# A cross-attention and mixture-of-experts kernel: the output bias added by VectorE instead of TensorE

## The chip, the core and the metric

The kernel runs on one core of one Trainium2 chip. The metric is the device time of one launch in microseconds (us). Engines are named as in the profile: PE is TensorE's matmuls and PEld its weight loads, DVE is VectorE, ACT is ScalarE, POOL is GpSimd, SP is SyncE. "L542" is line 542 of the kernel.

## The reference, cut to what matters

```
# x (8, 256, 256); ctx (8, 120, 256); 16 heads of 16; 8 experts
x = x + xattn(layernorm(x), ctx, ctx, ...)     # attention, ends in  out @ Wo.T + bo
x = x + ffn(layernorm(x), ...)                 # each row goes to one of 8 experts

def xattn(query, key, value, ..., Wo, bo, ...):
    ...
    out = einsum('bhqk,bkhd->bqhd', attn, v).reshape(Bq, Tq, D)
    return out @ Wo.T + bo

def ffn(x, router_w, router_b, expert_w, expert_b):
    logits = hs @ router_w + router_b
    ...                                        # argmax picks the expert, its softmax value is the gate
    out = gate * (hs @ expert_w[idx] + expert_b[idx])
```

The change is about `bo`, a vector of 256 floats, the same for every row.

## The kernel before

Eight batches b of 256 rows go through one software pipeline. Rows lie on the 128 partitions, so a batch is two tiles (TH = 2) of 128 rows by D = 256. Every engine runs its own instruction list, written out by hand, over iterations i = -1 to 7 with eight steps f = 0 to 7 in each. In iteration i four batches are in work: A = i + 2 (first layernorm, queries, keys, values), M = i + 1 (row maxima of the scores), i itself (scores, exponential, product with the values) and C = i - 1 (normalisation, output projection, residual), R = i - 2 (second layernorm, router). Engines wait for each other by semaphores: `v_mx` (DVE's maxima are done), `v_kL` and `v_qL` (the low parts of keys and queries), `p_op` (the output projection is in PSUM).

What one iteration does around the change, in the order of each engine:

- PE: step 4 scores (L500, L504), step 5 queries of A (L434), step 6 scores for the maxima of M (L474, L478), step 7 the values' product (L515), then `c_project(C)` (L542, L544), then `turn_max(M)` (L487, which waits for `v_mx`), the keys of the next batch (L434), the router's ranks; in the next iteration step 0 scores (L500, L504), step 1 `a_values` (L434, `w_nat,ctxs`, which waits for `v_kL`), and `c_out_turn` (L528).
- DVE: step 2 `maxima(M, 0)` (L1085), step 4 `ln1_stats(A + 1)` (L960, L963, L965), step 5 the router's logits (L1020 to L1030), `ln1_apply(A + 1)` (L979) and `queries_low(A)` (L1013), step 6 `maxima(M, 1)` (L1085), step 7 `route_choice`, `residual(C)` (L1103, then statistics L960 to L965), `keys_low(A + 1)` (L988), then small operations.
- POOL: powers -0.5 of the variances for both layernorms (`rsqrt1`, L338; `rsqrt2`, L362), and DMAs that scatter rows to their experts. In iteration -1 it also makes the bias operand (`output_bias`, L341 to L358), in iteration 1 it clears 4 tiles for the experts' bias (`bias_operands`, L328 to L332).

In iteration 7 `c_project(6)` stands in step 5, behind the scores. `c_project` puts two tiles into PSUM. An fp32 product is two matmul records in the trace for each of the two 128-row slices of the contraction (four L544 records for each tile), and ahead of them stands one bf16 matmul L542 with all ones as weights against `bo3`, whose rows 0, 32 and 64 hold the three bf16 parts of `bo`. DVE's L1103 adds the product to x in SBUF.

Behind the loop the last batches run mixed with the experts' blocks: 30 blocks of 128 rows, each read back from DRAM (SP), transposed (PE, L598), copied (ACT), multiplied (PE, L612, L614), gated (DVE, L1118) and stored by POOL's indirect DMA (L376). The projection of the last batch, `c_project(7)`, and its residual stand there, and POOL runs `store_block(0)` right before `rsqrt2(7)`.

Of the kernel before, what the change touches and what calls it, by code (L numbers as in the profile page):

```python
# [7 lines left out]
BF16 = mybir.dt.bfloat16  # L8
# [7 lines left out]
P = 128  # L16
# [4 lines left out]
def xattn_moe_kernel(nc, x, ctx_in, masks_in, Wq, Wk, Wv, Wo, bq_bk, bv, bo,  # L21
# [32 lines left out]
    with es:  # L54
# [56 lines left out]
        hT = sb("hT", [P, KC, T])  # L111
        utri = sb("utri", [P, P], BF16)
        onesb = sb("onesb", [P, P], BF16)
        bo3 = sb("bo3", [P, D], BF16)
        bor = sb("bor", [P, 2, D])
        tri8 = sb("tri8", [P, E, E])
        j128 = sb("j128", [P, E, NS])
        jblk = sb("jblk", [P, NBP[0]])
# [55 lines left out]
        for n in ("d_w0 d_w1 d_w2 d_w3 d_e d_bqk d_mk d_bv d_bias d_z0 d_z1 d_c0 d_c1 d_sc0 d_sc1 d_ebs d_ebp "  # L174
                  "c_pool c_late c_ebp c_warm c_dve a_T a_mk a_kbH a_kbL "
                  "g_r1 g_r2 p_xT p_q p_k p_v p_st p_pv p_mx p_T p_ot p_on p_op p_hT p_lg "
                  "a_tT a_xT a_qH a_kH a_exp a_oT a_hT a_hn a_le "
                  "v_ve1 v_xn v_qL v_kL v_va v_mx v_on v_x1 v_ve2 v_nb v_lc v_oh "
                  "a_ov g_bo p_rk v_slot v_be a_eb v_eb p_bT a_bT a_ob p_by v_by "
                  "dve").split() + [f"d_x{b}" for b in range(B)] + [f"d_hb{i}" for i in range(HR)] + [f"d_o{i}" for i in range(HR)]:  # L180
            s(n)

# [33 lines left out]
        def _(sp):  # L216
# [9 lines left out]
            sp.dma_start(rb_b[:, :], router_b.partition_broadcast(P)).then_inc(s("d_bias"), 16)  # L226
            sp.dma_start(eb[:, :], expert_b).then_inc(s("d_bias"), 16)
            sp.dma_start(r_nat[:, :, :], router_w.rearrange("(k p) e -> p k e", p=P)).then_inc(s("d_bias"), 16)
            for n in range(3):
                sp.dma_start(bo_b[32 * n:32 * n + 1, :], bo.rearrange("(o d) -> o d", o=1)).then_inc(s("d_bias"), 16)  # L230
            sp.wait_ge(s("d_w2"), 16)
            for b in range(2, B):
                load(b)
# [45 lines left out]
        def _(pool):  # L279
# [57 lines left out]
                    pool.wait_ge(s("v_xn"), b)  # L337
                pool.tensor_tensor(rs1[:, :], ve1[:, :], mhalf[:, :], ALU.pow).then_inc(s("g_r1"), 1)  # L338

            def output_bias():  # L340
                n = s("g_bo")  # L341
                pool.wait_ge(s("d_bias"), 16 * 6)
                pool.memset(bo3[:, :], 0.0).then_inc(n, 1)
                pool.wait_ge(n, 1)
                pool.tensor_copy(bo3[0:1, :], bo_b[0:1, :]).then_inc(n, 1)
                pool.tensor_copy(bo3[32:33, :], bo_b[32:33, :]).then_inc(n, 1)
                pool.tensor_copy(bo3[64:65, :], bo_b[64:65, :]).then_inc(n, 1)
                pool.wait_ge(n, 4)
                pool.tensor_tensor(bor[32:33, 0, :], bo_b[32:33, :], bo3[32:33, :], ALU.subtract).then_inc(n, 1)
                pool.tensor_tensor(bor[64:65, 0, :], bo_b[64:65, :], bo3[64:65, :], ALU.subtract).then_inc(n, 1)  # L350
                pool.wait_ge(n, 6)
                pool.tensor_copy(bo3[32:33, :], bor[32:33, 0, :]).then_inc(n, 1)
                pool.tensor_copy(bo3[64:65, :], bor[64:65, 0, :]).then_inc(n, 1)
                pool.wait_ge(n, 8)
                pool.tensor_tensor(bor[64:65, 1, :], bor[64:65, 0, :], bo3[64:65, :], ALU.subtract).then_inc(n, 1)
                pool.wait_ge(n, 9)
                pool.tensor_copy(bo3[64:65, :], bor[64:65, 1, :]).then_inc(n, 1)
                pool.wait_ge(n, 10)  # L358

            def rsqrt2(b):  # L360
                pool.wait_ge(s("v_ve2"), b + 1)
                pool.tensor_tensor(rs2[:, tiles(b)], ve2[:, :], mhalf[:, :], ALU.pow).then_inc(s("g_r2"), 1)  # L362
# [19 lines left out]
            for i in ITER:  # L382
                A, C = i + 2, i - 1
                if i == -1:
                    late_constants()
                if 0 <= i - 3:
                    scatter(i - 3)
                if A + 1 < B:
                    rsqrt1(A + 1)
                if i == -1:  # L390
                    output_bias()
                if i == 1:
                    bias_operands()
                if 0 <= C < B:
                    rsqrt2(C)
# [18 lines left out]
        def _(pe):  # L414
# [120 lines left out]
            def c_project(b):  # L535
                pe.wait_ge(s("a_oT"), b + 1)
                if b == 0:
                    pe.wait_ge(s("d_w3"), 16)
                    pe.wait_ge(s("c_late"), NLATE)
                    pe.wait_ge(s("g_bo"), 10)  # L540
                for h in range(TH):
                    pe.matmul(PJk[:, h, :], onesb[:, :], bo3[:, :], start=True, stop=False)  # L542
                    for k in range(KC):
                        t = pe.matmul(PJk[:, h, :], oT[:, k, h * P:(h + 1) * P], w_nat[:, 3, k, :],  # L544
                                      start=False, stop=(k == KC - 1))
                t.then_inc(s("p_op"), 1)

            def c_hidden_turn(b):
# [3 lines left out]
            def c_logits(b):  # L552
                pe.wait_ge(s("a_hT"), b + 1)
                if b == 0:
                    pe.wait_ge(s("d_bias"), 16 * 6)
                if b >= 1:
                    pe.wait_ge(s("v_lc"), b)
                    pe.wait_ge(s("v_slot"), b)
                if b == FB[1]:
                    pe.wait_ge(s("v_be"), 2)  # L560
                for h in range(TH):
                    t = full(RT_LG[:, h, :], lambda k: hT[:, k, h * P:(h + 1) * P], lambda k: r_nat[:, k, :])
                t.then_inc(s("p_lg"), 1)

            def r_ranks(b):
                pe.wait_ge(s("v_oh"), b + 1)
                if b >= 1:
                    pe.wait_ge(s("v_slot"), b)
                for h in range(TH):
                    t = TH * b + h  # L570
                    pe.matmul(RT_RK[:, h, :], utri[:, :], oh[:, t, :], start=True, stop=False)
                    m = pe.matmul(RT_RK[:, h, :], onesb[:, :], cum[:, place_in_cum(t), :], start=False, stop=True)
                if b + 1 in FB:
                    m = pe.matmul(RT_TOT, onesb[:, :], cum[:, place_in_cum(t) + 1, :], start=True, stop=True)
                m.then_inc(s("p_rk"), 1)
# [162 lines left out]
        def _(act):  # L738
# [108 lines left out]
                a.then_inc(s("a_kbL"), 1)  # L847

            def split_expert_bias():
                act.wait_ge(s("d_bias"), 16 * 6)  # L850
                act.activation(ebs[:, 0, :], eb[:, :], ACT.Copy).then_inc(s("a_eb"), 1)

            act.dma_start(w_nat[:, 1, :, :], Wk).then_inc(s("d_w1"), 16)
# [87 lines left out]
        def _(v):  # L941
# [32 lines left out]
            def ln1_apply(b):  # L974
# [5 lines left out]
                                        ALU.subtract, ALU.mult)  # L980
                i.then_inc(s("v_xn"), 1)

            def keys_low(bn):
                v.wait_ge(s("a_kH"), KC * (bn + 1))
                if bn >= 2:
# [114 lines left out]

            def residual(b):
                v.wait_ge(s("p_op"), b + 1)
                v.tensor_tensor(xr[:, tiles(b), 0:D], xr[:, tiles(b), 0:D], PJk, ALU.add).then_inc(s("v_x1"), 1)  # L1103
                v.wait_ge(s("v_x1"), b + 1)
                if b >= 1:
                    v.wait_ge(s("v_nb"), b)
                ln_stats(b, st2, xr[:, tiles(b), C_MEAN:C_MEAN + 2], ve2, "v_ve2")
# [28 lines left out]
            for i in ITER:  # L1136
                A, M, C, R = i + 2, i + 1, i - 1, i - 2
                isA, isM, isS, isC, isR = (0 <= n < B for n in (A, M, i, C, R))
                for f in range(NF):
# [20 lines left out]
                    if f == 4:  # L1160
                        if i == -1:
                            maxima(M, 1)
                            values(A)
                        if A + 1 < B:
                            ln1_stats(A + 1)
                    if f == 5:
# [107 lines left out]
```

## Time and profile before

| | |
|---|---|
| time, median of 3 runs | 224.46 us (223.33 to 224.56) |
| the profiled execution | 221.88 us, of which the span of its instructions 220.0 us |
| granted TensorE clock, mean | 0.973 |
| busy: PE, PEld, DVE, ACT, POOL | 194.4, 135.8, 137.5, 124.6, 69.4 us |
| L542 (ones by bias parts) | 16 matmuls, mean record 277 ns |
| L544 (output projection) | 64 matmuls, mean record 380 ns |
| L1103 (residual add) | 8 instructions, mean 674 ns |

Matmuls overlap in the pipeline, so a record is longer than the time that a matmul takes from the next; the distance from start to start tells the latter. Idle time in square brackets is the time that the engine stood idle before an instruction, and what ended it. A group "x4" starts at the first of its four instructions and ends with the last.

### The profile page before, as it was taken

To read this page: it belongs to the slowest core of one execution; us is meant where nothing else is said; L and a number is where in the kernel's file an instruction comes from. 1 tells how busy PE (TensorE), PEld (TensorE's weight loads), DVE (VectorE), ACT (ScalarE), POOL (GpSimd) and SP (SyncE) were. 2 spreads that over 40 slices of the span, in tenths; PEclk is the share of its full clock that TensorE was granted. 3 is DMA by queue.
4 is the path that set the end of the run, shared out by engine and by line. 5 is a ranking of instruction groups with operands and counts; after the bars stand their busy time and mean duration, and the time that the engine had idled before them with its cause. 6 is when DMAs were issued, how large, how long until landed. Compare 5 with 4: busy or idle time off the path is not lost.

```text
span 220.0 us, 4891 instructions
## 1 busy us (share of the span) xinstructions
PE 194.4 (88%) x1656; PEld 135.8 (62%) x1656; DVE 137.5 (62%) x479; ACT 124.6 (57%) x273; POOL 69.4 (32%) x106
## 2 busy tenths in 40 slices
PE   7999898999999999999999899889698982799930
PEld 2757464666685766757668455556587671588720
DVE  4577756688668877985973774884757580223420
ACT  2575684584784676487477556376636370645810
POOL 7321810050110230131040040040164667466672
PEclk9999999999999999999999999999999999589995
DMA  6899500005000010010010000014850215551110
GB/s 215 276 347 354 173 1 3 3 3 197 4 0 0 4 51 0 0 53 0 3 50 0 3 24 27 0 48 114 227 151 7 102 55 172 144 153 47 60 40 0
DMA packets 14650, 17.12 MB, mean 78 GB/s; under 512 B 2687, under 2 KB 12958, under 8 KB 14625
## 3 DMA queue, kind: packets, MB, share of 16 engines
q1 hardware_dynamic: 11698, 10.67, 16.3%
q0 software_dynamic: 2208, 4.24, 5.4%
q10 hardware_dynamic: 720, 1.91, 2.4%
q8 instruction: 14, 0.23, 0.5%
q14 instruction: 10, 0.07, 0.1%
HBM read 10.43 MB, written 8.21 MB: 85 GB/s over the span
## 4 chain that ended last, share of the span: by engine, by line
PE 57%; DVE 13%; issue 10%; POOL 7%; another core or an unknown queue 4%; ACT 4%; DMA 2%; POOLq 1%; SPq 0%; ACTq 0%; DVEq 0%
PE ps L434 14%; PE ps L504 6%; POOL out_dram L376 6%; PE ps L500 6%; PE ps L544 6%; PE ps L515 5%; DVE nm L1085 5%; PE ps L474 5%; PE ps L428 4%; PE ps L478 3%; DMA ctxs<-in_ctx_dram 2%; ACT pr L763 2%; PE ps L614 2%; PE ps L528 1%
## 5 line engine op out<-in xcount | busy, mean ns | idle before, releaser
L763 ACT ACTIVATE pr<-ps 120x512 f32<-120x512 f32 x64 | 33.0, 603 | 18.9 <-PE ps L504 18.9
L1085 DVE TENSOR_REDUCE nm<-ps 128x4 bf16<-128x480 f32 x64 | 37.5, 649 | 6.8 <-PE ps L478 5.8
L376 POOL DMA_INDIRECT out_dram<-ob,hb x30 | 29.5, 983 | 16.0 <-issue 11.2
L614 PE MATMUL ps<-ew,bT 128*128 x120 | 32.6, 397 | 0.0
L1118 DVE SCALAR_TENSOR_TENSOR ob<-ps,hb,ob 128x256 f32<-128x256 f32 x30 | 14.1, 482 | 26.8 <-PE ps L614 12.2
L362 POOL TENSOR_TENSOR rs<-ve,mhalf 128x2 f32<-128x2 f32 x8 | 5.7, 707 | 69.0 <-DVE ve L965 68.6
L743 ACT ACTIVATE bT<-ps 128x256 f32<-128x256 f32 x30 | 11.3, 380 | 23.6 <-PE ps L598 12.8
L614 PEld LDWEIGHTS ps<-ew,bT 128*128 128x128 f32 x120 | 21.9, 202 | 1.9
L371 POOL DMA_INDIRECT rows_by_expert<-xr,slot x16 | 16.0, 1000 | 13.8 <-DVE slot L1050 11.0
L338 POOL TENSOR_TENSOR rs<-ve,mhalf 128x2 f32<-128x2 f32 x8 | 5.6, 706 | 46.2 <-DVE ve L965 43.2
L769 ACT ACTIVATE ou<-ps 128x512 f32<-128x512 f32 x16 | 9.6, 597 | 17.5 <-PE ps L515 17.5
L500 PE MATMUL ps<-tT,sel 128*120 128x512 bf16 x64 | 17.8, 390 | 1.1 <-ACT tT L812 0.7
L598 PE MATMUL ps<-identf,hb 128*128 128x128 f32 x60 | 12.3, 292 | 6.7 <-ACT bT L743 6.7
L515 PE MATMUL ps<-pr,va 120*32 120x256 f32 x256 | 17.3, 385 | 0.5 <-ACT pr L763 0.3
L749 ACT ACTIVATE ob<-hb 128x256 f32<-128x256 f32 x30 | 17.7, 593 | 0.0
L474 PE MATMUL ps<-idm,tT 128*128 128x480 bf16 x64 | 16.6, 367 | 0.9 <-DVE nm L1085 0.4
L544 PE MATMUL ps<-w_nat,oT 128*128 128x256 f32 x64 | 16.0, 380 | 0.0
L434 PE MATMUL ps<-xT,w_nat 128*128 128x256 f32 x64 | 15.7, 387 | 0.0
L598 PEld LDWEIGHTS ps<-identf,hb 128*128 128x128 f32 x60 | 8.2, 152 | 10.6 <-issue 8.9
L960 DVE BATCH_NORM_STATS2 st<-xr 128x6 f32<-128x256 f32 x32 | 12.0, 416 | 2.2 <-DMA xr<-in_x_dram 1.9
L434 PEld LDWEIGHTS ps<-xT,w_nat 128*128 128x128 f32 x64 | 11.6, 190 | 2.0 <-ACT xT L786 0.5
L544 PEld LDWEIGHTS ps<-w_nat,oT 128*128 128x128 f32 x64 | 11.0, 192 | 1.9
(143 smaller groups left out, 374.4 us busy)
## 6 DMA issues: line engine op xcount, KB each, us to landing
hb<-rows_by_expert SPq DMA_DIRECT2D x30, 130.0 KB, 2.5
rows_by_expert<-zer SPq DMA_DIRECT2D x2, 1040.0 KB, 8.7
xr<-in_x_dram SPq DMA_DIRECT2D x8, 256.0 KB, 4.8
ew<-in_expert_w_dram SPq DMA_DIRECT2D x2, 1024.0 KB, 9.7
ctxs<-in_ctx_dram ACTq DMA_DIRECT2D x1, 840.0 KB, 5.7
out_dram<-ob,hb POOLq DMA_INDIRECT x30, 2.6
w_nat<-in_Wk_dram ACTq DMA_DIRECT2D x1, 256.0 KB, 3.3
w_nat<-in_Wq_dram ACTq DMA_DIRECT2D x1, 256.0 KB, 4.3
```

Of the source, the lines that this page charges most:

```text
L371: pool.indirect_dma_start(rows_d[p], bass.IndirectOffsetOnAxis(ap=slot[:, t:t + 1], axis=0), xr[:, t, :], None).then_inc(s(f"d_sc{p}"), 16)
L376: pool.indirect_dma_start(out_rows, bass.IndirectOffsetOnAxis(ap=hb[:, j % HR, C_ID:C_ID + 1].bitcast(U32), axis=0), ob[:, j % HR, :], Non ...
L434: t = pe.matmul(out_ap, l(k), r(k), start=(k == 0), stop=(k == KC - 1))
L474: pe.matmul(SC[r][:, 0:G * S], tT[:, b, 0, h * P:(h + 1) * P], idm[:, :].unsqueeze(1).to_broadcast([P, G, S]), start=True, stop=False)
L500: pe.matmul(SC[r][0:S, :], sel[:, 2 * r + e, :], tT[:, b, :, :], start=True, stop=False)
L515: t = pe.matmul(OVg[32 * j:32 * j + 32, g % 2, :], va[:, b % 3, G * g + j, :, :], pr[:, 2 * (g % 2) + j // 2, j % 2, :], start=True, stop= ...
L544: t = pe.matmul(PJk[:, h, :], oT[:, k, h * P:(h + 1) * P], w_nat[:, 3, k, :], start=False, stop=(k == KC - 1))
L598: t = pe.transpose(TURN[j % 2][:, k * P:(k + 1) * P], hb[:, j % HR, k * P:(k + 1) * P], identf[:, :])
L614: t = pe.matmul(prod, bT[:, m % 3, k, :], ew[:, k, bass.ds(e, 1), :], start=False, stop=(k == KC - 1))
L749: act.activation(ob[:, m % HR, :], row[:, 0:D], ACT.Identity, scale=row[:, C_DEV:C_DEV + 1], bias=row[:, C_MEAN:C_MEAN + 1]).then_inc(s("a ...
L763: act.activation(pr[:, r, :, :], SC[r][0:S, :], ACT.Exp, scale=SCALE).then_inc(s("a_exp"), 1)
L1085: v.tensor_reduce(nm[:, b % 2, h, :, 2 * r:2 * r + 2], SC[r][:, 0:G * S].rearrange("p (c e s) -> p c e s", c=KC, e=2), AX_X, ALU.max, nega ...
```

## The change

The two bf16 matmuls in `c_project` go, and with them POOL's `output_bias`, the tiles `bo3` and `bor` and PE's wait for them. `bo` is loaded once to all 128 partitions (128 KB written) instead of three times to one partition (1 KB each). DVE adds it to x of batch i in step 4 of iteration i, the iteration ahead of the one whose step 7 adds the projection. `c_late`, which `c_project(0)` waited for, is now waited for in `r_ranks(0)`.

```
-            for n in range(3):
-                sp.dma_start(bo_b[32 * n:32 * n + 1, :], bo.rearrange("(o d) -> o d", o=1)).then_inc(s("d_bias"), 16)
+            sp.dma_start(bo_b[:, :], bo.partition_broadcast(P)).then_inc(s("d_bias"), 16)
...
-            def output_bias():            # POOL: 1 memset, 6 copies, 3 subtractions, called in iteration -1
...
-                if i == -1:
-                    output_bias()
...
                 if b == 0:
                     pe.wait_ge(s("d_w3"), 16)
-                    pe.wait_ge(s("c_late"), NLATE)
-                    pe.wait_ge(s("g_bo"), 10)
                 for h in range(TH):
-                    pe.matmul(PJk[:, h, :], onesb[:, :], bo3[:, :], start=True, stop=False)
                     for k in range(KC):
                         t = pe.matmul(PJk[:, h, :], oT[:, k, h * P:(h + 1) * P], w_nat[:, 3, k, :],
-                                      start=False, stop=(k == KC - 1))
+                                      start=(k == 0), stop=(k == KC - 1))
...
             def r_ranks(b):
                 pe.wait_ge(s("v_oh"), b + 1)
+                if b == 0:
+                    pe.wait_ge(s("c_late"), NLATE)
...
+            def output_bias(b):           # DVE
+                if b == 0:
+                    v.wait_ge(s("d_bias"), 16 * 4)
+                v.wait_ge(s("v_xn"), b + 1)
+                v.tensor_tensor(xr[:, tiles(b), 0:D], xr[:, tiles(b), 0:D],
+                                bo_b[:, :].unsqueeze(1).to_broadcast([P, TH, D]), ALU.add).then_inc(s("v_bo"), 1)
...
             def residual(b):
                 v.wait_ge(s("p_op"), b + 1)
+                v.wait_ge(s("v_bo"), b + 1)
...
                     if f == 4:
                         if i == -1:
                             maxima(M, 1)
                             values(A)
+                        if isS:
+                            output_bias(i)
                         if A + 1 < B:
                             ln1_stats(A + 1)
```

## Rows read from the trace of the kernel before

**Rows 1.** Busy time by stretch: engine, busy us (instructions); then granted clock, DMA share.
```profile
core 0: us, PE busy (x) PEld busy (x) DVE busy (x) ACT busy (x) POOL busy (x), PEclk, DMA share, GB/s
78.10:96.20 18.10, 18.02 (x183) 12.54 (x179) 14.13 (x53) 12.20 (x27) 3.86 (x5) 1.00 0.05 18
187.50:194.50 7.00, 5.84 (x19) 4.88 (x20) 1.84 (x4) 3.82 (x10) 3.69 (x4) 0.51 0.66 177
```

**Rows 2.** Timeline of PE, iteration 3: start us, us, instruction, count [idle before].
```profile
87.15 0.28 PE L542 MATMUL ps<-bo,onesb 128*128 128x256 bf16 x1
87.27 1.03 PE L544 MATMUL ps<-w_nat,oT 128*128 128x256 f32 x4
88.14 0.27 PE L542 MATMUL ps<-bo,onesb 128*128 128x256 bf16 x1
88.25 1.03 PE L544 MATMUL ps<-w_nat,oT 128*128 128x256 f32 x4
...
92.50 1.12 PE L434 MATMUL ps<-w_nat,ctxs 128*120 128x256 f32 x4
93.46 1.34 PE L528 MATMUL ps<-identf,ou 128*128 128x128 f32 x8
```

**Rows 3.** Timeline of PE's weight loads, iterations 3 and 4.
```profile
89.20 0.20 PEld L487 LDWEIGHTS ps<-identb,nm 128*8 128x8 bf16 x4 [0.33 <-issue]
...
98.54 0.13 PEld L500 LDWEIGHTS ps<-tT,sel 128*120 128x120 bf16 x1 [0.30 <-DVE nm L1085]
```

**Rows 4.** Timeline of DVE, iterations 3 and 4.
```profile
84.37 0.74 DVE L979 TENSOR_SCALAR xn<-xr,mv,rs 128x256 f32<-128x256 f32 x2
85.89 0.88 DVE L1013 SCALAR_TENSOR_TENSOR qL<-ps,bqk,qH 128x256 fp32r<-128x256 f32 x2 [0.79 <-ACT qH L791]
86.69 2.34 DVE L1085 TENSOR_REDUCE nm<-ps 128x4 bf16<-128x480 f32 x4
...
89.89 0.67 DVE L1103 TENSOR_TENSOR xr<-xr,ps 128x512 f32<-128x512 f32 x1
...
91.74 0.59 DVE L988 SCALAR_TENSOR_TENSOR kL<-ps,bqk,kH 128x120 f32<-128x120 f32 x2
...
96.13 2.35 DVE L1085 TENSOR_REDUCE nm<-ps 128x4 bf16<-128x480 f32 x4 [0.51 <-issue]
98.40 0.74 DVE L960 BATCH_NORM_STATS2 st<-xr 128x6 f32<-128x256 f32 x2
...
101.28 0.17 DVE L1020 TENSOR_TENSOR lg<-ps,rb_b 128x16 f32<-128x16 f32 x1 [1.65 <-PE ps L434]
```

**Rows 5.** Timeline of POOL: start, iteration 1 and behind the loop.
```profile
22.20 0.39 POOL L345 CAST bo<-bo_b 1x256 bf16<-1x256 f32 x1
...
47.19 1.93 POOL L330 MEMSET ebp<- 128x512 f32 x4
...
163.09 1.00 POOL L376 DMA_INDIRECT out_dram<-ob,hb  x1 [0.30 <-issue]
164.55 0.72 POOL L362 TENSOR_TENSOR rs<-ve,mhalf 128x2 f32<-128x2 f32 x1 [0.46 <-issue]
```

**Rows 6.** Timeline of DVE: iterations -1 and 1.
```profile
21.91 0.83 DVE L979 TENSOR_SCALAR xn<-xr,mv,rs 128x256 f32<-128x256 f32 x2 [0.82 <-POOL rs L338]
...
47.15 2.44 DVE L979 TENSOR_SCALAR xn<-xr,mv,rs 128x256 f32<-128x256 f32 x2 [0.81 <-POOL rs L338]
49.90 0.88 DVE L1013 SCALAR_TENSOR_TENSOR qL<-ps,bqk,qH 128x256 fp32r<-128x256 f32 x2 [0.32 <-ACT qH L791]
...
50.70 2.34 DVE L1085 TENSOR_REDUCE nm<-ps 128x4 bf16<-128x480 f32 x4
```

**Rows 7.** Timeline of PE's weight loads: iterations 0, 1 and 5.
```profile
24.08 0.71 PEld L434 LDWEIGHTS ps<-w_nat,ctxs 128*120 128x120 f32 x4 [0.91 <-DVE kL L988]
...
53.14 0.20 PEld L487 LDWEIGHTS ps<-identb,nm 128*8 128x8 bf16 x4 [0.33 <-DVE nm L1085]
...
125.39 0.22 PEld L487 LDWEIGHTS ps<-identb,nm 128*8 128x8 bf16 x4 [0.33 <-issue]
```

**Rows 8.** Timeline of PE in the tail.
```profile
188.66 0.66 PE L598 MATMUL ps<-identf,hb 128*128 128x128 f32 x2 [5.65 <-ACT bT L743]
```

More of the change, by code:

```diff
@@ L113, in xattn_moe_kernel @@
         onesb = sb("onesb", [P, P], BF16)
-        bo3 = sb("bo3", [P, D], BF16)
-        bor = sb("bor", [P, 2, D])
         tri8 = sb("tri8", [P, E, E])
@@ L178, in xattn_moe_kernel @@
                   "v_ve1 v_xn v_qL v_kL v_va v_mx v_on v_x1 v_ve2 v_nb v_lc v_oh "
-                  "a_ov g_bo p_rk v_slot v_be a_eb v_eb p_bT a_bT a_ob p_by v_by "
+                  "a_ov v_bo p_rk v_slot v_be a_eb v_eb p_bT a_bT a_ob p_by v_by "
                   "dve").split() + [f"d_x{b}" for b in range(B)] + [f"d_hb{i}" for i in range(HR)] + [f"d_o{i}" for i in range(HR)]:
@@ L338, in rsqrt1 @@
                 pool.tensor_tensor(rs1[:, :], ve1[:, :], mhalf[:, :], ALU.pow).then_inc(s("g_r1"), 1)
-            def output_bias():
[L341 to L358, printed above, removed]
             def rsqrt2(b):
@@ L554, in c_logits @@
                 if b == 0:
-                    pe.wait_ge(s("d_bias"), 16 * 6)
+                    pe.wait_ge(s("d_bias"), 16 * 4)
                 if b >= 1:
@@ L849, in split_expert_bias @@
             def split_expert_bias():
-                act.wait_ge(s("d_bias"), 16 * 6)
+                act.wait_ge(s("d_bias"), 16 * 4)
                 act.activation(ebs[:, 0, :], eb[:, :], ACT.Copy).then_inc(s("a_eb"), 1)
```

## The prediction

> **What bounds the kernel now.** I read the busy time by stretch first. In a full iteration of the loop PE is busy 18.02 of 18.10 us at the full clock of 2.4 GHz, DVE 14.13, ACT 12.20, POOL 3.86 [rows 1]. So time taken from PE there can count, and work given to DVE can hide. But DVE's 4 us of idle time say little; what counts is where they lie. So I then read the timelines of PE and of DVE over one iteration, looking for each place where PE waits for a semaphore of DVE, and for how long DVE has been done when PE gets there. The chain of waits confirms that nearly all of the loop hangs on PE; from 158 us on it runs through POOL's indirect DMAs, waits with no known source, and short pieces of every engine.
>
> **What PE saves.** A record of L542 lasts 0.28 us, but that overlaps its neighbours; from start to start the second of the pair takes 88.14 to 88.25, 0.11 us [rows 2]. The first one is different. From its start to that of the second L542 are 0.99 us, for one bf16 matmul and four records of L544. It comes right after the 32-column matmuls of L515, where PE has to begin anew. Four fp32 records of the same length that come right after such small matmuls, with no bf16 matmul ahead, are L434 on `w_nat,ctxs`: 92.50 to 93.46, 0.96 us [rows 2]. So the first fp32 matmul after a change of shape costs extra, and the first L542 hides it. With L542 gone the first tile takes 0.96 instead of 0.99: 0.03 saved. An iteration gives PE 0.03 + 0.11 = 0.14 us, seven times (batches 0 to 6). `c_project(7)` comes after full-size matmuls, so it saves 2 x 0.11 = 0.22. Sum: 7 x 0.14 + 0.22 = 1.20 us.
>
> The Trainium skill ("TensorE: Matmul & The Clock Gate", Back-to-back issue gap) gives 262 cycles at 2.4 GHz for a matmul with 256 columns, 0.109 us; by it 16 matmuls would give back 1.75 us. The trace agrees for the second of each pair and not for the first, so I keep 1.20.
>
> **What of it PE can keep.** Two waits for DVE follow. `turn_max` waits for `v_mx`: DVE's last maximum ends at 86.69 + 2.34 = 89.03, PE's load of L487 starts at 89.20 [rows 3, 4]. How long does a semaphore take? Where PE truly waits for a maximum (L500 at 98.54), DVE had ended at 96.13 + 2.35 = 98.48: 0.06 us. So PE could come 89.20 - 89.03 - 0.06 = 0.11 earlier before it must wait. `a_values` waits for `v_kL`: done at 91.74 + 0.59 = 92.33, PE starts at 92.50, again 0.11 [rows 2, 4]. DVE's chain from `qL` over the maxima, L1103 and `kL` has no gap that PE could shorten; it starts when ACT has copied the queries, which PE released before `c_project`. So of 0.14 only about 0.11 passes. The iterations 2 and 4 read the same, with 0.12. Three iterations: 0.35 us. In iteration 5 there is no `kL`, but the last maximum ends at 125.27 and L487 starts at 125.39 [rows 7]: 0.06 passes. In iterations 6 and 7 no such wait is near: 0.14 each.
>
> **What DVE gets.** A 128x512 fp32 add: L1103, the same shape with one input in PSUM, takes 0.67 us [rows 4]. The trace has no such add from SBUF alone. The bounds are the 0.74 of two scalings of 128x256 in SBUF and about 0.59, which is 0.67 less the 0.08 by which neighbours on DVE overlap (98.48 against 98.40) [rows 4]. I take 0.67 long, 0.59 of DVE's time, eight times, 4.7 us in all. It stands between the maxima and L960. Behind it L960, POOL's power and L979 come later by 0.59, but between L965 and the router's logits DVE stands idle 1.65 us [rows 4], and another 0.79 before `qL` [rows 4]. In iterations 2 to 6 it costs nothing; if that cover were gone it would cost 0.59 each, 3 us. In iterations 0 and 7 DVE waits for PE behind the place of the add as well, longer than 0.59: nothing either.
>
> **Iteration 1** has no router yet, so no such gap. There L979 takes 2.44 us instead of 0.74, because POOL clears the experts' bias tiles (L330, 1.93 us) at the same time [rows 5, 6]: POOL starts right after the power, and the first scaling ends only when POOL has finished. The add moves the power by 0.59, and the memsets behind it, and so the end of L979 from 49.59 to 50.18. `qL` started at 49.90 with 0.32 of idle time before it [rows 6]; now it starts at 50.18 - 0.08 = 50.10, 0.20 later. The maxima end at 50.70 + 2.34 + 0.20 = 53.24, and L487, before at 53.14 [rows 7], at 53.30. Iteration 1 becomes 0.16 us longer, and PE's 0.14 are lost in the wait. Bounds: -0.04 (if the memsets don't move with it, that is all the leeway PE has there) and +0.5.
>
> **POOL and the start.** POOL's 10 instructions of the bias (0.39 us for a copy [rows 5], 4.7 us in all) run beside L979 of batch 2, which takes 0.83 against 0.74 for the same pair elsewhere [rows 4, 6], and PE truly waits for the `kL` behind it, 0.91 us [rows 7]. That gives 0.09 back. The rest of POOL's bias work releases nobody before 51 us. The broadcast writes 128 KB instead of 3 KB around 5 us, while the DMA engines are busy with weights; at the 350 GB/s that the page shows there, it takes 0.4 us of them. The next loads are needed more than 1.5 us after they land: nothing. SP saves two issues and then waits for a weight load anyway.
>
> **Behind the loop.** `c_project(7)` ends 0.22 earlier, and with it L1103 and the variance. POOL's power `rsqrt2(7)` at 164.55 stands behind a store that ends at 164.09, and POOL's next instruction follows a DMA by 0.30 [rows 5]. So it can start at 164.39: 0.16 of 0.22 passes.
>
> **Sum.** -0.09 (start) + 0.16 (iteration 1) - 0.35 (2 to 4) - 0.06 (5) - 0.28 (6, 7) - 0.16 (behind the loop) = -0.78 us. The profiled execution of 221.88 (span 220.0) becomes 221.1. It ran 2.6 us below the median; the effect is the same for both, so 224.46 becomes 223.7, -0.35%. A measurement of this kernel can tell about 0.5%, 1.1 us, from no change: I forecast no change that can be told.
>
> **The rivals.**
> - *Everything passes.* If DVE's chain starts earlier as well, or its leeway is larger than I read, and iteration 1 doesn't suffer: 1.20 + 0.09 = 1.29, 223.2 us, -0.57%. The 0.11 at two waits in three iterations speak against it.
> - *The tail shifts, for the better.* Between 187.5 and 194.5 PE runs at 1.2 GHz (granted 0.51), busy 5.84 of 7.00 us [rows 1], after it stood idle 5.65 us before 188.66 [rows 8]. At full clock the same work would take half, 2.9 us less. That idle time hangs on how SP's loads and POOL's stores (1.3 us apart) interleave, and any shift can change it. Without the slow stretch: -0.78 - 2.9, 220.8 us.
> - *The tail shifts, for the worse* (my rival on the other side). One more such stretch, or as much again in that one, costs 2.9: +2.1, 226.6 us. It decides from 1.9 us of extra stall on, two thirds of a stretch. For it: the 0.6 to 0.9 us that reach the tail early may meet another store; against it: all engines there shift nearly alike.
> - *The add is not 0.67.* L979 beside POOL's memsets went from 0.37 for one scaling to about 2.1. If the new add were held up so in every iteration it would take 2.1; the idle 1.65 + 0.79 = 2.44 still cover it, and only iteration 1 would pay, 1.4 more: 225.1 us, +0.3%. In a full iteration POOL is busy only 3.86 of 18.10 us [rows 1]. The Trainium skill ("GPSIMD Engine Reference", Key points) says that GpSimd shares its SBUF interfaces with VectorE and contends with an instruction that has two SBUF inputs; this add is one, while L1103 with its PSUM input is not. What iteration 1 shows is a one-input case.
>
> **Chances.** Forecast as worked out 0.50; everything passes 0.14; tail better 0.15; tail worse 0.13; slow add 0.08. Faster by over 0.5%: 0.14 + 0.15 = 0.29. Slower: 0.13. Same: 0.58. The range: the three runs of before, 223.33 to 224.56, moved by -0.78 are 222.6 to 223.8, and the bounds of iteration 1 (-0.20 to +0.34 against what I took) make the likeliest case 222.4 to 224.1; to hold 8 in 10 it takes in everything-passes and the slow add, and the nearer half of both tails: 221.9 to 225.3.
>
> **What would show it.** L542 gone; the first four L544 of a pair 0.96 us, not 0.87; a full iteration 17.99 instead of 18.10, with PE marked as waiting for DVE's `kL` or maximum; eight adds of 0.67; L979 of iteration 1 still 2.4 and `qL` 0.2 late; L979 at the start 0.74. I am wrong if the iterations shrink by 0.14 or more, if the add shows over 1 us, or if the span to 160 us changes by the forecast 0.6 but the end doesn't: then the tail decided.

## The result, and the profile after

```
this    222.77 us median (221.48 to 224.01, 13 runs)
before  224.42 us median (222.99 to 226.75, 13 runs)
ratio of this to before 0.9946, 95% interval 0.9923 to 0.9970
```

By the ratio of the runs the change is faster by 0.54% (0.30 to 0.77%), 1.2 us; the two medians lie 1.65 us apart. The 0.5% named as the limit of what can be told lies within the interval, and no change does not. Forecast were 223.7 us and -0.35%.

The page of the changed kernel (first lines, and the group of the output projection: busy, mean ns of one | idle before):

```profile
PE 195.3 (88%) x1640; PEld 136.9 (62%) x1640; DVE 141.5 (64%) x487; ACT 124.6 (56%) x273; POOL 65.0 (29%) x96
...
PEclk9999999999999999999999999999889997579995
...
L516 PE MATMUL ps<-w_nat,oT 128*128 128x256 f32 x64 | 16.5, 402 | 0.0
```

Its windows, columns as in [rows 1]: one full iteration, then two stretches behind the loop.

```profile
77.37:95.44 18.07, 17.96 (x180) 12.52 (x176) 14.74 (x54) 12.14 (x27) 4.01 (x5) 1.00 0.06 21
158.20:161.60 3.40, 3.40 (x10) 2.79 (x10) 0.83 (x3) 1.32 (x3) 1.86 (x2) 0.50 0.75 210
...
185.50:195.70 10.20, 7.75 (x24) 5.89 (x24) 1.99 (x5) 4.13 (x10) 5.87 (x7) 0.50 0.60 162
```

A full iteration went from 18.10 to 18.07 us; DVE is busier by 0.61 there and nobody pays for it. The stretch at half clock (1.2 GHz) near 186 us, 6.8 us long before, is 10.2 us long here. And the granted clock fell to half near 158 us too, which it did not in the profiled execution before. So the two profiled executions alone mislead: 222.83 us for this one, against 221.88 for the one before, which was below all 13 timed runs of before. To read the change, I split the trace at points that every run has: the first weight load of each turn of the maxima (L487 before, L462 after; the first one ends iteration -1), and the start of POOL's last power, `rsqrt2(7)`.

```
us                iteration 0     1     2     3     4     5     6   | to rsqrt2(7) | from there to the end
before                  16.29 16.90 17.96 18.10 18.09 18.10 15.87 | 23.29        | 55.50
this                    16.20 16.87 17.84 18.07 18.07 18.11 15.73 | 24.59        | 56.16
forecast difference     -0.09 +0.16 -0.12 -0.11 -0.12 -0.06 -0.14 | -0.30        |
measured difference     -0.09 -0.04 -0.12 -0.03 -0.02 +0.01 -0.14 | +1.30        | +0.66
```

DVE's timeline in iterations 3 and 4 of the changed kernel, to set beside [rows 4]:

```profile
83.67 0.73 DVE L953 TENSOR_SCALAR xn<-xr,mv,rs 128x256 f32<-128x256 f32 x2
85.19 0.88 DVE L994 SCALAR_TENSOR_TENSOR qL<-ps,bqk,qH 128x256 fp32r<-128x256 f32 x2 [0.79 <-ACT qH L765]
85.99 2.34 DVE L1066 TENSOR_REDUCE nm<-ps 128x4 bf16<-128x480 f32 x4
...
91.06 0.59 DVE L969 SCALAR_TENSOR_TENSOR kL<-ps,bqk,kH 128x120 f32<-128x120 f32 x2
...
97.67 0.68 DVE L961 TENSOR_TENSOR xr<-xr,bo_b 128x512 f32<-128x512 f32 x1
98.27 0.74 DVE L934 BATCH_NORM_STATS2 st<-xr 128x6 f32<-128x256 f32 x2
...
100.56 0.18 DVE L1001 TENSOR_TENSOR lg<-ps,rb_b 128x16 f32<-128x16 f32 x1 [1.06 <-PE ps L409]
```

The add takes 0.68 us (0.67 was taken), and the idle time ahead of the router's logits went from 1.65 to 1.06: it swallowed 0.59, as worked out. The 0.79 ahead of `qL` is untouched.

PE's weight loads at the ends of iterations 2 and 3, to set beside [rows 3]:

```profile
70.37 0.20 PEld L462 LDWEIGHTS ps<-identb,nm 128*8 128x8 bf16 x4 [0.34 <-DVE nm L1066]
...
88.44 0.23 PEld L462 LDWEIGHTS ps<-identb,nm 128*8 128x8 bf16 x4 [0.40 <-issue]
```

In iteration 2 the load now follows DVE by 0.05 us. In iteration 3 the last maximum ends at 85.99 + 2.34 = 88.33, and the load starts 0.115 behind it (0.11 by the rounded rows), not 0.06. Nothing looks like a wait here ("issue"), and yet PE gained only 0.03. That is the first open point; the second is the end, the third iteration 1, where +0.16 was forecast and -0.04 came.

### The profile page after: what moved, and what is told of

Read it like the earlier page. It is cut to its first block, busy times and chain, and to the rows that moved or that the text cites. A ratio compares the mean times of both kernels' runs of the same rounds, so it can differ in the third digit from the quotient of the medians.

```text
span 221.1 us, 4863 instructions
## 1 busy us (share of the span) xinstructions
PE 195.3 (88%) x1640; PEld 136.9 (62%) x1640; DVE 141.5 (64%) x487; ACT 124.6 (56%) x273; POOL 65.0 (29%) x96
## 4 chain that ended last, share of the span: by engine, by line
PE 73%; DVE 11%; issue 5%; ACT 3%; DMA 2%; POOL 1%; another core or an unknown queue 1%; POOLq 1%; SPq 0%; ACTq 0%; DVEq 0%
PE ps L409 14%; PE ps L588 13%; PE ps L516 7%; PE ps L479 6%; PE ps L490 6%; PE ps L475 6%; DVE nm L1066 5%; PE ps L449 5%; PE ps L403 4%; PE ps L572 4%; PE ps L453 3%; DMA ctxs<-in_ctx_dram 2%; ACT pr L737 2%; PE ps L586 2%; PE ps L503 1%
## 5 line engine op out<-in xcount | busy, mean ns | idle before, releaser
L588 PE MATMUL ps<-ew,bT 128*128 x120 | 34.2, 413 | 0.0
L588 PEld LDWEIGHTS ps<-ew,bT 128*128 128x128 f32 x120 | 22.8, 209 | 2.1
L516 PE MATMUL ps<-w_nat,oT 128*128 128x256 f32 x64 | 16.5, 402 | 0.0
L516 PEld LDWEIGHTS ps<-w_nat,oT 128*128 128x128 f32 x64 | 12.2, 199 | 4.2 <-DVE qL L994 2.1
## 6 DMA issues: line engine op xcount, KB each, us to landing
ew<-in_expert_w_dram SPq DMA_DIRECT2D x2, 1024.0 KB, 10.2
```

The lines of the kernel that those rows point to most:

```text
L588: t = pe.matmul(prod, bT[:, m % 3, k, :], ew[:, k, bass.ds(e, 1), :], start=False, stop=(k == KC - 1))
```

## The experiments

**One part at a time.** The chip of these four runs the kernel before in 217.01 us (one run), that of the comparison above in 224.42. There is one profiled execution of each; two of them have the half-clock stretch near 159 us, so the whole times can't be set against each other, and the iterations are read instead.

`no_add`: the changed kernel without the adds. The output bias is missing from its result.

```
- v.tensor_tensor(xr[:, tiles(b), 0:D], xr[:, tiles(b), 0:D], bo_b..., ALU.add).then_inc(s("v_bo"), 1)
  ...
- v.wait_ge(s("v_bo"), b + 1)            # in residual
```

> The changed kernel without VectorE's bias add and its wait (the output then lacks the bias; nothing else is left out). Measure: from the first to the last load of L487 of the kernel before (its turn_max of batches 0 and 7): 121.31 us before, 120.89 after. My theory: the adds hide in idle time and the saving of PE is capped by DVE's old chain from the low queries over the maxima; then iterations 2 to 5 stay as after (-0.12, -0.03, -0.02, +0.01 against before) and only iteration 1 gains, to 120.8. Rival: the adds delay DVE's chain; then iterations 3 to 5 go to about -0.13 each and the stretch to 120.5.

`add_only`: the kernel before with the broadcast load and the adds, its matmuls kept. The bias is added twice.

```
+ sp.dma_start(bo_b[:, :], bo.partition_broadcast(P)).then_inc(s("d_bias"), 16)
+ output_bias(i)                         # on DVE, where the changed kernel has it
  pe.matmul(PJk[:, h, :], onesb[:, :], bo3[:, :], start=True, stop=False)   # stays
```

> The kernel before with the bias matmuls and POOL's bias work kept, plus the broadcast load and VectorE's eight adds (the bias is added twice). My theory (adds hidden): the stretch between the same two loads stays 121.3 except for iteration 1, where the scaling beside POOL's memsets ends later: +0.0 to +0.2. Rival (the add is on the path): +0.05 or more in each of iterations 2 to 6, 121.6 or more. The Wv load should land 1.4 us later than before (10.1 instead of 8.7) as in the changed kernel, without moving PE.

`drop_first` and `drop_second`: the kernel before without the bf16 matmul of the first tile, or of the second. Half of the rows lack the bias.

```
  for h in range(TH):
-     pe.matmul(PJk[:, h, :], onesb[:, :], bo3[:, :], start=True, stop=False)
+     if h == 1:                         # drop_second: h == 0
+         pe.matmul(PJk[:, h, :], onesb[:, :], bo3[:, :], start=True, stop=False)
```

> The kernel before without the first of each pair of bias matmuls only (rows 0 to 127 of each batch lack the bias). My theory: a bf16 matmul behind the small matmuls hides the extra cost of the first fp32 one, so c_project from the last L515 to L487 shortens by 0.03, not 0.12. Rival: it shortens by 0.12. From the first to the last L544 of the pair: 1.625 before, then 1.72.

> The kernel before without the second of each pair only (rows 128 to 255 lack the bias). c_project shortens by 0.11 in every batch by both theories; what of it arrives at L487 tells the leeway that DVE leaves: 0.11 if the leeway is 0.11 or more, 0.03 to 0.06 if the wait costs 0.06 more than I read, as the changed kernel suggests (there L487 starts 0.115 after the last maximum in iterations 3 to 5 instead of 0.054).

```
us                iteration 0     1     2     3     4     5     6   | to rsqrt2(7) | to the end | time
no_add                  16.21 16.87 17.85 18.05 18.08 18.12 15.75 | 22.92        | 49.23      | 214.98
add_only                16.30 17.05 17.97 18.10 18.09 18.10 15.86 | 24.96        | 49.24      | 217.02
drop_first              16.30 16.86 17.95 18.07 18.10 18.10 15.85 | 23.14        | 49.26      | 215.03
drop_second             16.30 16.88 17.86 18.03 18.07 18.12 15.77 | 24.72        | 49.23      | 216.41
```

PE's timeline of `drop_first` in iteration 3:

```profile
86.72 1.13 PE L545 MATMUL ps<-w_nat,oT 128*128 128x256 f32 x4
87.69 0.27 PE L543 MATMUL ps<-bo,onesb 128*128 128x256 bf16 x1
87.80 1.03 PE L545 MATMUL ps<-w_nat,oT 128*128 128x256 f32 x4
```

and of `drop_second`:

```profile
86.66 0.28 PE L543 MATMUL ps<-bo,onesb 128*128 128x256 bf16 x1
86.78 1.89 PE L545 MATMUL ps<-w_nat,oT 128*128 128x256 f32 x8
```

In `drop_first` the first tile takes 86.72 to 87.69, 0.97 us, where [rows 2] has 0.99 with one matmul more: 0.02 saved. `drop_second` saves 0.11 (from the last product with the values to the last matmul of the projection 1.94 us instead of 2.06). So the two matmuls are worth 0.13 us in a pair, not 2 x 0.11; of the 0.14 of the forecast, 0.13 held. The first fp32 matmul behind the small ones takes 0.32 us to the next start instead of 0.22. The Trainium skill ("TensorE: Matmul & The Clock Gate", Back-to-back issue gap) would give 0.109 us for each; that fits the second and is far from the first.

Of the 0.11 that `drop_second` saves on PE, the iterations keep 0.10 in number 2, 0.07 in 3, 0.02 in 4 and nothing in 5. In the last three PE's load starts 0.116 behind DVE's maximum: the second case of its expectation.

`no_add` has the iterations of the changed kernel to 0.02 us: the adds cost the loop nothing there. And the loop's gain is no bigger without them, so what PE saves is stopped by waits that were there before. The gain that was expected in iteration 1 (120.8 us from the first to the last turned maxima) did not come: 16.87 and 120.93, against 16.87 and 120.89 with the adds. `add_only` pays in iteration 1 alone, 17.05 against 16.90: there the +0.16 of the forecast came (+0.15).

**Where the rest is.** Four kernels on one chip, which runs the kernel before in 216.32 us. `again_after` is the changed kernel; `no_add_t` is `no_add`, timed eleven times.

> The changed kernel once more, timed against the kernel before on one chip. Theory: the loop and the start give the change 0.65 us, the rest of what was measured (1.2 us) is which executions had an additional half-clock stretch, so the ratio should lie between 0.994 and 0.999. Rival: the change also does something for the end; then the ratio stays at 0.9946 or below. First turned maxima (L462) to the last one: 120.9 us again, against 121.3 before.

> The changed kernel without the eight DVE adds and the wait on them: the output bias is missing from the result. Theory: the adds lie in DVE's idle time, so the time is that of the changed kernel within 0.1 us in the loop (120.92 us between the first and the last turned maxima); ratio to the kernel before within 0.2% of that of the changed kernel. Rival, each add costs the critical chain a part of its 0.68 us: 0.2 us or more for each, then this one is 1.5 us or more (0.7%) below the changed kernel.

`warm_tail` gives PE work to do in a gap behind the loop:

```
  block_step(1)
+ keep_warm(5)                           # dummy matmuls of 512 columns into a free PSUM bank
  c_norm_turn(B - 1)
```

> The changed kernel with five dummy 512-column matmuls on PE behind block 1, in the 1.4 us in which PE waits for the normalised rows of the last batch. Theory: the half-clock stretch of 3.4 us near 158 us comes after PE has been idle here, costs about 1.3 us, and is taken away, so no stretch at half clock lies between 150 and 185 us in the profile, and the ratio to the kernel before is 0.3 to 0.6% lower than that of the changed kernel if a good part of its executions have the stretch. Rival: the stretch is not due to this idle time; then it stays or comes as often, and the time is the same or up to 0.2 us more.

`wait_moved` moves one of PE's waits:

```
  if isC and i < B - 1:
+     read("v_slot", R - 1)
      read("v_qL", A)
      c_project(C)
  ...
  if isM:
-     read("v_slot", R - 1)
      turn_max(M)
```

> The changed kernel with PE's wait for the slots of an earlier batch moved from just ahead of the turn of the maxima to ahead of the output projection of the same iteration. Theory: in iterations 3, 4 and 5 the wait for the last maximum is then a part of the weight load itself and not an instruction of its own, and the load starts 54 ns behind the maximum instead of 116; each of the three iterations is 0.05 to 0.06 us shorter (18.01 instead of 18.07), the span between the first and the last turned maxima 120.72 instead of 120.89. Rival: the 116 ns come from something else (the projection ends later than it seems), and the starts stay at 115 to 117 ns.

```
before        216.32 us median (215.21 to 217.07, 28 runs)
again_after   214.92 us median (12 runs), ratio 0.9949 (0.9920 to 0.9979)
no_add_t      214.67 us median (11 runs), ratio 0.9930 (0.9903 to 0.9958)
warm_tail     214.52 us median (12 runs), ratio 0.9926 (0.9901 to 0.9950)
wait_moved    214.81 us (one run)

us                iteration 0     1     2     3     4     5     6   | to rsqrt2(7) | to the end
again_after             16.21 16.85 17.84 18.05 18.07 18.11 15.74 | 22.92        | 49.24
no_add_t                16.20 16.87 17.84 18.05 18.07 18.11 15.75 | 22.91        | 49.23
warm_tail               16.19 17.04 17.84 18.06 18.06 18.12 15.73 | 22.92        | 49.24
wait_moved              16.19 16.85 17.84 17.99 18.02 18.05 15.73 | 22.93        | 49.23
```

The ratio came again, 0.9949. It lies inside the expected 0.994 to 0.999 and next to the 0.9946 of the rival, so it does not decide between them. `no_add_t` lies 0.2% below `again_after`; both intervals are wider than that, and its loop is the same, so a price of the adds of 0.7% is excluded and one of nothing fits.

The weight loads of `wait_moved` at the ends of iterations 2 and 3:

```profile
71.05 0.20 PEld L462 LDWEIGHTS ps<-identb,nm 128*8 128x8 bf16 x4 [0.34 <-DVE nm L1066]
...
89.03 0.20 PEld L462 LDWEIGHTS ps<-identb,nm 128*8 128x8 bf16 x4 [0.34 <-DVE nm L1066]
```

That settles the first point. From iteration 3 on `turn_max` has two waits ahead of it (`v_slot` joins `v_mx`). The trace then shows `v_mx` as an instruction of its own on PE's sequencer, 51 ns long, which is released and only then followed by the load: 0.115 us behind DVE. With the other wait elsewhere the load itself waits and starts 0.052 behind. Iterations 3, 4 and 5 became 0.06, 0.05 and 0.06 shorter (18.05 to 17.99, 18.07 to 18.02, 18.11 to 18.05), and the mark changed from "issue" to the name of the one waited for.

On the end: from `rsqrt2(7)` on all eight profiled executions on these two chips take 49.23 to 49.26 us. There, whatever is gained up to that point reaches the end whole. Up to that point, three of the profiles so far hold a half-clock stretch of 3.4 us near 160 us (the changed kernel's first one, `add_only`, `drop_second`), and their stretch "to rsqrt2(7)" is 24.59, 24.96 and 24.72 us; the others have 22.92 to 23.29. PE in the changed kernel's first profile:

```profile
158.63 1.91 PE L588 MATMUL ps<-ew,bT 128*128 x4
160.33 2.53 PE L516 MATMUL ps<-w_nat,oT 128*128 128x256 f32 x8
```

and in `again_after`:

```profile
159.00 1.02 PE L588 MATMUL ps<-ew,bT 128*128 x4
159.86 1.89 PE L516 MATMUL ps<-w_nat,oT 128*128 128x256 f32 x8
```

With the same kernel (on two chips) this costs 24.59 - 22.92 = 1.67 us. The timed runs of this chip show the same two kinds: the spans of before are 14 of 213.3 to 214.1 and 14 of 214.8 to 215.2 us, those of `again_after` 8 of 212.4 to 213.4 and 4 of 214.0 to 214.3. Group against group the change is worth 0.75 us (medians 213.55 and 212.8) and 1.0 us (215.0 and 214.0). The mean granted clock agrees with two kinds: 0.971 to 0.973 in the upper groups, 0.974 to 0.981 in the lower ones. It is no proof of the place: `wait_moved`, with no stretch near 160 us, has 0.974. The 12 runs of `warm_tail` all lie between 212.4 and 213.4. Its dummies on PE:

```profile
155.60 1.24 PE L600 MATMUL ps<-warm 128*128 128x512 bf16 x5
157.13 0.66 PE L403 MATMUL ps<-identf,on 128*128 128x128 f32 x4 [0.29 <-DVE on L1078]
```

The gap in which PE waits for the normalised rows was 1.37 us, and is 0.29. At four in twelve, twelve runs without one of the upper group would come about once in 130 times; at five in 23, the share with the eleven of `no_add_t` counted in, once in 19. The ratio, 0.9926, is 0.23% below that of `again_after`, and 0.3 to 0.6% was expected. The idle 1.37 us alone doesn't bring the stretch either: `before`, `no_add` and `again_after` have it too, and no stretch.

**The size of the change without the stretch, and its first term.** These four ran on a chip that takes 223.88 us for the kernel before. `before_warm` and `warm_again` are the kernels before and after with the same five dummies.

> The kernel before with five dummy matmuls on PE behind block 1, as in warm_tail. On the chip of the last comparison the executions of the kernel before fell into two groups of 14, with spans of 213.3 to 214.1 and 214.8 to 215.2 us, those of the changed kernel into 8 of 212.4 to 213.4 and 4 of 214.0 to 214.3. Theory: the upper group is the additional half-clock stretch near 158 us; the dummy matmuls take it away here too, all executions lie in one group, and the ratio to the kernel before is 0.996 to 0.998. The changed kernel with the same dummies (warm_again) is then 0.7 to 0.9 us below this one, which is the change without the stretch. Rival: the group is decided elsewhere, and about half of the executions stay 1.4 us above the others.

> The changed kernel with the five dummy matmuls, once more beside before_warm. Theory: 0.7 to 0.9 us (0.35 to 0.4%) below before_warm, of which the steps between the first and the last turned maxima give 0.42 us. Rival: what the measured 0.5% has above the sum of the loop was the half-clock stretch alone, then it is 0.4 us or less.

`all_three` is `warm_tail` with `wait_moved` and

```
- if i == 1:
+ if i == 0:
      bias_operands()                    # POOL's memsets for the experts' bias
```

> The changed kernel with the dummy matmuls, the wait for the slots moved ahead of the projection, and POOL's preparation of the expert bias one iteration earlier. Theory: 0.2 us less than warm_again in iterations 3 to 5 (18.01 instead of 18.07 us each), nothing from the expert bias in iteration 1, since PE still has its own work there (16.85 instead of 16.87), and if POOL's memset now holds a DVE instruction in iteration 0 that step grows by up to 0.2 us. Ratio to the kernel before 0.991 to 0.993. Rival: the gain of the moved wait is taken back behind the loop, where POOL's rows decide; then it equals warm_again.

`prep_late` is the kernel before, with

```
- if i == -1:
+ if i == 0:
      output_bias()                      # POOL's ten instructions for the three bf16 parts
```

> The kernel before with POOL's ten instructions for the three bf16 parts of the bias one iteration later. Tests the first term of the forecast alone. Theory: those instructions held DVE's normalisation at 21.9 us to 0.83 us; with them gone from there it takes 0.73, and the step from the first to the second turned maxima is 16.20 us as in the changed kernel, not 16.29 to 16.30. Rival: the 0.09 us come from the removed matmuls or another cause, then the step stays at 16.29.

```
before        223.88 us median (222.91 to 225.46, 27 runs)
before_warm   223.30 us median (12 runs), ratio 0.9978 (0.9949 to 1.0006)
warm_again    222.43 us median (10 runs), ratio 0.9928 (0.9903 to 0.9954)
all_three     222.69 us median (12 runs), ratio 0.9939 (0.9917 to 0.9961)
prep_late     223.97 us (one run)

us                iteration 0     1     2     3     4     5     6   | to rsqrt2(7) | to the end
before_warm             16.28 16.88 17.97 18.10 18.11 18.10 15.85 | 23.27        | 57.45
warm_again              16.18 17.03 17.83 18.06 18.06 18.11 15.74 | 22.91        | 57.36
all_three               16.18 16.85 17.85 17.99 18.00 18.06 15.73 | 22.92        | 56.67
prep_late               16.20 16.89 17.96 18.09 18.11 18.10 15.86 | 23.26        | 57.42
```

With the dummies in both, the change is worth 223.30 - 222.43 = 0.87 us, 0.39%, and by the ratios 0.50% (0.9928 against 0.9978), each with some 0.25% on either side (so the 0.50% has nearly 0.4% on either side, and zero is only just outside). The expected 0.7 to 0.9 fits the medians; that the dummies alone help before is not shown (-0.22%, with zero in the interval). One of the 12 runs of `before_warm` lies at a span of 223.8 us, the others at 220.9 to 222.2. And on this chip the runs of before show no two groups (spans 221.0 to 223.6, no gap), so the test of the stretch is `warm_tail`'s alone.

`prep_late` has the 16.20 of the changed kernel in iteration 0. DVE's scaling in it:

```profile
22.22 0.74 DVE L979 TENSOR_SCALAR xn<-xr,mv,rs 128x256 f32<-128x256 f32 x2 [0.82 <-POOL rs L338]
```

0.74 instead of 0.83 [rows 6]: with POOL's bias work moved away from it, the whole first term is there.

`all_three` is 0.36 us ahead of `warm_again` at `rsqrt2(7)` (0.18 in iteration 1, 0.18 in 3 to 5), but its median is 0.26 above. The part from there to the end took 56.67 to 57.45 us in the four profiles of this chip (55.50 and 56.16 in the first comparison), with waits of up to 5.3 us on ACT whose releaser the trace only calls "remote", and 0.36 us can't be told in that. Its ratio, 0.9939, is outside the expected 0.991 to 0.993 and fits the rival (equal to `warm_again`). It beat the kernel before (0.6%); that it beats the changed kernel is not shown. In iteration 0, where the memsets stand now, nothing grew (16.18).

**Iteration 1.** Six runs have the add and the memsets there. In `again_after`, DVE and POOL:

```profile
47.75 1.33 DVE L953 TENSOR_SCALAR xn<-xr,mv,rs 128x256 f32<-128x256 f32 x2 [0.80 <-POOL rs L335]
49.91 0.87 DVE L994 SCALAR_TENSOR_TENSOR qL<-ps,bqk,qH 128x256 fp32r<-128x256 f32 x2 [0.83 <-ACT qH L765]
```

```profile
47.80 2.21 POOL L327 MEMSET ebp<- 128x512 f32 x4
```

in `warm_again`:

```profile
47.03 2.44 DVE L954 TENSOR_SCALAR xn<-xr,mv,rs 128x256 f32<-128x256 f32 x2 [0.81 <-POOL rs L335]
49.39 0.86 DVE L995 SCALAR_TENSOR_TENSOR qL<-ps,bqk,qH 128x256 fp32r<-128x256 f32 x2
50.17 2.33 DVE L1067 TENSOR_REDUCE nm<-ps 128x4 bf16<-128x480 f32 x4
...
52.56 0.20 PEld L462 LDWEIGHTS ps<-identb,nm 128*8 128x8 bf16 x4 [0.62 <-DVE nm L1067]
```

```profile
47.08 1.93 POOL L327 MEMSET ebp<- 128x512 f32 x4
```

and in `all_three`, the memsets gone from there:

```profile
47.06 0.73 DVE L954 TENSOR_SCALAR xn<-xr,mv,rs 128x256 f32<-128x256 f32 x2 [0.81 <-POOL rs L335]
49.21 0.88 DVE L995 SCALAR_TENSOR_TENSOR qL<-ps,bqk,qH 128x256 fp32r<-128x256 f32 x2 [1.42 <-ACT qH L766]
```

The scaling and the memsets (0.52 us each where nothing holds them) hold each other up, and who goes first differs from run to run. If POOL goes on to the end (four memsets in 1.93), the scaling takes 2.44, `qL` loses its idle time and the iteration is 17.03 to 17.05 (`add_only`, `warm_tail`, `warm_again`). If DVE gets in between (1.33, and POOL 2.21) or late (2.26 in the first profile after), `qL` still waits for ACT or is 0.03 late, and the iteration is 16.85 to 16.87. Without memsets it is 16.85: with `qL` in time PE sets the end. The Trainium skill ("GPSIMD Engine Reference", Key points) tells of shared SBUF interfaces and of contention with a DVE instruction that is in a 2-port mode or has two SBUF inputs. The rows show it for a scaling with one input; in which mode that runs, no trace here shows. The two-input add met no POOL instruction in any of its eight places, so no run here shows what it would cost beside one.

## Why the forecast was nearly right

*What is the same as forecast.* The total to `rsqrt2(7)`, start of the count at the first turned maxima: 144.60 us before, 143.79 in `again_after`, -0.81 us; the forecast was -0.78. The measured medians differ by 0.87 (with the dummies), 1.40 and 1.65 us. The path is the one described, and so are the add (0.68), its cover, PE's 0.13 a pair, the start (-0.09, shown by `prep_late`), and iterations 2, 6 and 7. The other forecast, no change that can be told, failed: the interval excludes no change in both comparisons (0.9946 and 0.9949). It had been drawn from -0.35%, and the measured ratios are larger than that by about the 0.2% treated below.

*What was off, each way.*
- "So PE could come 89.20 - 89.03 - 0.06 = 0.11 earlier": this step failed. The 0.06 is the delay of a load that itself holds the wait (L500). L487 has two waits from iteration 3 on and comes 0.115 behind DVE. So iterations 3 to 5 gave 0.04 of the forecast 0.29 (0.06 in `again_after`; forecast 0.11, 0.12 and 0.06). With the wait moved they give 0.23 (0.11, 0.07, 0.05): the leeway was then nearly what had been read, and `wait_moved` is the kernel of which the forecast was nearly true. Its iteration 3 has the 17.99 named as the sign; the changed kernel has 18.05 to 18.07.
- "qL ... 0.20 later", iteration 1 +0.16: right where POOL isn't interrupted (+0.15 in `add_only`, 17.03 against 16.88 in the dummy pair), wrong where it is (-0.04). "Bounds: -0.04 (if the memsets don't move with it ...)" had the number, with another reason.
- "So it can start at 164.39: 0.16 of 0.22 passes": all of it passed. POOL in `again_after`:

```profile
162.61 1.00 POOL L353 DMA_INDIRECT out_dram<-ob,hb  x1 [0.30 <-issue]
163.83 0.72 POOL L339 TENSOR_TENSOR rs<-ve,mhalf 128x2 f32<-128x2 f32 x1 [0.23 <-DVE ve L939]
```

The power follows the store by 0.22 us, less than the 0.30 taken from two stores in a row, and waits for DVE. Iteration 7 and the part behind the loop together gave 0.37 (23.29 to 22.92), forecast 0.30. (In [rows 5] the power stood 0.46 behind the store.)
- "it takes 0.4 us of them": the load of the values' weights beside the broadcast went from 2.9 to 4.4 us from issue to landing, 1.5 longer, and to 5.4 in `warm_again`. Before, it landed 2.5 us ahead of its first use (8.7 and 11.19); now 0.1 to 1.2 us ahead, and in `warm_again` PE waited for it:

```profile
w_nat<-in_Wv_dram ACTq DMA_DIRECT2D x1, 256.0 KB, 4.4
```

```profile
10.99 1.12 PE L409 MATMUL ps<-w_nat,ctxs 128*120 128x256 f32 x4 [0.23 <-DMA w_nat<-in_Wv_dram]
```

That reached nobody: from PE's first product for the queries (8.77 us there, 9.36 before) to the first turned maxima are 10.58 or 10.59 us in all the kernels here. But "nothing" held because of leeway that was nearly used up. What lies ahead of that product varies by 0.9 us between executions, with and without the broadcast, and the marks leave it out.

The misses cancel in `again_after`: 0.23 forecast too much in iterations 3 to 5, 0.21 too little in iteration 1 and 0.07 too little from iteration 7 on. -0.78 was right for a partly wrong reason.

*The rivals.* "Everything passes" had the size that the first comparison showed (-0.57%), and is refuted as a mechanism: iterations 3 to 5 didn't shrink by 0.14, and 0.81 us arrived, not 1.29. The slow add didn't occur. Both tail rivals named the right kind of thing, a half-clock stretch that comes or not, but they looked for it at 187.5 us [rows 1, 8] and as an effect of the change. There the changed kernel's first profile did have one that is 3.4 us longer, and the part behind `rsqrt2(7)` took 0.66 us more, not 2.9; in `warm_again`, with 6.8 us of it again, that part took 57.36 us, longer than either. So the price of 2.9 us was not seen in any profile. The stretch at 158 us came in one profiled execution of the changed kernel and not in another, and cost 1.67 us. It can account for 0.81 us looking like 1.1: where `warm_tail` ran, before was in the upper group in 14 of 28 runs, this in 4 of 12. The difference in shares, 0.17, times the 1.45 us between the groups is 0.25 us; with the 0.87 us of the mean of the two group differences that is 1.12 us, 0.52%, where 0.51% was measured. Whether the change makes the stretch rarer, or the draw did, stays open: 14 of 28 against 4 of 12 is no proof (with `no_add_t`, where one of 11 lies at 214.1, it is 5 of 23). That it has to do with PE's idle time at 154.8 to 157.5 is supported by the 12 runs of `warm_tail`, and not by more.

## What to carry to other kernels

When you read how much earlier an engine could start before a wait binds, take the semaphore's delay from that very instruction in a place where it truly waits, and count the waits ahead of it: here a second wait ahead of one weight load cost 0.06 us in each of three iterations, and with it most of what they could have gained. Removing work from the busiest engine gives at most the leeway to the next wait in each iteration (from nothing to 0.12 of 0.13 here), so look for those waits first. And when a change is worth less than a clock stretch that comes in some executions, compare marks inside the trace, or remove the stretch on both sides, before you believe a median.

## What the hardware showed that was not expected

- The first fp32 matmul after 32-column matmuls takes 0.32 us to the next start, the following ones 0.216; a bf16 matmul ahead of it hides 0.10 of its own 0.12.
- A wait as an instruction of its own ahead of a weight load costs 0.115 us from DVE's end, within the load 0.052.
- A memset of POOL and a one-input scaling of DVE on SBUF hold each other up, and which of them waits varies between runs: the pair of scalings took 0.73 us alone and 1.33, 2.26 or 2.44 beside the memsets.
- A load of 256 KB beside a broadcast of one 1 KB row to 128 partitions landed 4.4 to 5.4 us after its issue, without it 2.9 to 3.2.
- PE's clock fell to half (1.2 GHz) at 158.2 us in one profiled execution of the changed kernel, after PE had stood idle for 1.37 us before 156.20 and 0.61 us before 157.46, and did not in the other. With five dummy matmuls in the first gap it fell there in none of the four profiles that have them; of the ten without them it fell in three, so that alone is weak. The Trainium skill ("TensorE: Matmul & The Clock Gate", Part 1: The HAM clock gate) says that the ramp varies from run to run, because the chip's watching isn't tied to the kernel's start; the profiles here show such a variation for the fall in the middle of a kernel too.
- Two chips differ by 3% (216.3 and 223.9 us for the kernel before), all of it behind `rsqrt2(7)`: 49.2 against 56.7 to 57.5 us. Between the first turned maxima and there, one kernel takes 143.95 us on the one (`warm_tail`) and 143.93 on the other (`warm_again`).
